# Value products of an attention in runs of two blocks

## The reference

```python
# attention a: one key and value head for all 16 query heads, D = 16
scores = jnp.einsum('bnhd,bmd->bhnm', q, k) / jnp.sqrt(jnp.float32(D))
attn = jax.nn.softmax(jnp.where(causal, -jnp.inf, scores), axis=-1)
out = jnp.einsum('bhnm,bmd->bnhd', attn, v).reshape(b, n, E) @ w_fc + b_fc
# attention b: own keys and values for each head, ALiBi
scores = jnp.einsum('bhqd,bhkd->bhqk', q, k) / scale + _alibi_bias(H, Tlen)[None]
out = jnp.einsum('bhqk,bhkd->bhqd', jax.nn.softmax(scores, axis=-1), v)
```

## Time and profile before

| | us |
|---|---|
| median of 3 runs | 1035.86 (1034.84 to 1036.69) |
| the profiled execution's own time | 1033.63 |
| its span | 1031.9 |
| busy in the span: TensorE, VectorE | 964.2 (93%), 760.6 (74%) |
| busy in the span: ScalarE, GpSimd | 570.4 (55%), 411.3 (40%) |

### The profile page before, as it was taken

How to read it: one execution, slowest core, us unless ns; L and a number is a source line. 1 busy time by engine, 2 the same in 40 slices (tenths; PEclk the granted TensorE clock), 3 DMA queues, 4 the chain that set the end, 5 groups by cost and what they waited for, 6 DMA issues and landing times.

```text
span 1031.9 us, 19370 instructions
## 1 busy us (share of the span) xinstructions
PE 964.2 (93%) x6370; PEld 613.2 (59%) x6370; DVE 760.6 (74%) x2132; ACT 570.4 (55%) x1078; POOL 411.3 (40%) x434
## 2 busy tenths in 40 slices
PE   4888999999889999999998989999999899999998
PEld 3433333333358889988886433333334588899887
DVE  6798999999256776447778979999992568764475
ACT  4525777777744335653354647777777533466332
POOL 3420634333435417625843102323225361374570
PEclk9879999999989999999999989999999999999999
DMA  4721212210105215733249523334401251266351
GB/s 142 193 46 30 47 44 44 44 44 9 49 26 203 80 47 173 181 122 120 67 116 218 118 36 69 61 70 77 76 13 44 84 173 53 82 190 160 117 183 48
DMA packets 66755, 95.40 MB, mean 92 GB/s; under 512 B 19669, under 2 KB 50821, under 8 KB 64599
## 3 DMA queue, kind: packets, MB, share of 16 engines
q1 hardware_dynamic: 46645, 52.74, 19.0%
q10 hardware_dynamic: 13100, 22.53, 8.6%
q0 software_dynamic: 6912, 18.88, 7.0%
HBM read 66.79 MB, written 26.67 MB: 91 GB/s over the span
## 4 chain that ended last, share of the span: by engine, by line
PE 71%; DVE 16%; issue 4%; DMA 3%; ACT 3%; POOL 2%; SPq 1%; ACTq 0%; DVEq 0%; POOLq 0%
PE o_ps L1101 13%; PE st_ps L1084 8%; PE su_ps L1043 7%; PE st_ps L293 7%; PE st_ps L294 7%; PE st_ps L295 7%; PE o_ps L1241 4%; PE st_ps L1043 4%; PE su_ps L1241 3%; DVE mab L1729 3%; PE su_ps L1147 3%; DVE unread L1725 3%; PE st_ps L1276 2%; DVE xn L1604 1%; PE su_ps L293 1%
## 5 line engine op out<-in xcount | busy, mean ns | idle before, releaser
L1446 ACT ACTIVATE pt<-st_ps 128x512 f32<-128x512 f32 (+1 forms) x584 | 312.0, 596 | 161.3 <-PE st_ps L1084 153.5
L1084 PE MATMUL st_ps<-qs,ks 99*128 99x512 bf16 (+9 forms) x768 | 211.8, 328 | 4.3 <-DMA qs<-nmx 2.4
L807 POOL TENSOR_SCALAR_AFFINE_SELECT pt<-pt 128x512 f32<-128x512 f32 x120 | 74.7, 641 | 311.7 <-ACT pt L1446 311.7
L1043 PE MATMUL su_ps<-ks,qs 102*128 102x512 bf16 (+7 forms) x538 | 155.2, 330 | 11.5 <-DVE mc L1725 4.5
L1101 PE MATMUL o_ps<-pt,vp 128*32 128x512 f32 (+3 forms) x1536 | 156.6, 505 | 0.0
L1725 DVE CUSTOM_DVE_ANT_0 unread<-su_ps,cst 128x384 f32<-128x384 f32 (+3 forms) x324 | 143.0, 479 | 16.2 <-PE su_ps L1043 15.5
L1729 DVE TENSOR_REDUCE mab<-su_ps 128x1 f32<-128x512 f32 (+2 forms) x181 | 118.6, 683 | 7.2 <-PE su_ps L1043 5.1
L1043 PEld LDWEIGHTS su_ps<-ks,qs 96*128 96x128 bf16 (+1 forms) x538 | 48.5, 98 | 122.4 <-DVE mab L1729 44.4
L888 POOL DMA_INDIRECT rows_in<-rows,source x80 | 79.1, 989 | 97.5 <-DVE source L1988 73.7
L1084 PEld LDWEIGHTS st_ps<-qs,ks 99*128 99x128 bf16 (+2 forms) x768 | 73.1, 98 | 63.5 <-ACT pt L1446 16.6
L1472 ACT CAST hh<-hf 128x512 fp32r<-128x512 f32 x64 | 39.7, 620 | 123.2 <-DVE hf L1943 123.2
(11 more groups left out here) (234 smaller groups left out, 1975.7 us busy)
## 6 DMA issues: line engine op xcount, KB each, us to landing
wu_raw<-w_units_dram SPq DMA_DIRECT2D x32, 384.0 KB, 3.2
outs<-rows_out ACTq DMA_DIRECT2D x40, 256.0 KB
q_parts<-hml SPq DMA_DIRECT2D x16, 384.0 KB, 3.1
wexp_raw<-w_units_dram SPq DMA_DIRECT2D x16, 384.0 KB, 6.5
inv<-inverses SPq DMA_DIRECT2D x128, 32.0 KB, 1.8
rows<-xn SPq DMA_DIRECT2D x8, 512.0 KB, 6.2
qs<-q_parts ACTq DMA_DIRECT2D x10, 384.0 KB
k_parts<-hml SPq DMA_DIRECT2D x8, 384.0 KB, 2.9
```

The lines of the kernel that those rows point to most:

```text
L807: pool.affine_select(block, block, [[0, 4], [1, P]], ALU.is_ge, 0.0, base=0, channel_multiplier=-1).then_inc(masked, 1)
L1043: last = pe.matmul(out_b[:, c0:c0 + width], query_columns(s, slice(0, rows), j0 + a, P * qt, P * qt + P), key_stack(l, s)(j0 + a)[0:rows, ...
L1084: last = pe.matmul(out_b[:, at:at + hi - lo], key_stack(l, s)(j)[0:rows, P * kt:P * kt + P], query_columns(s, slice(0, rows), j, lo, hi), ...
L1446: act.activation(exponentials(S, q)[:, j, 0:width_of(s, q)], bank[KM_BANKS[i % len(KM_BANKS)]][:, 0:width_of(s, q)], ACT.Exp, scale=1 / np ...
```

## The change

The value products are given in runs. Instead of one block at a time, two blocks behind the start of the piece, the order in each step is: block 0 alone behind block 2, blocks 1 and 2 behind block 4, 3 and 4 behind block 6, 5 and 6 behind block 8, and 7 and 8 behind block 1 of the next step, each time behind piece 1. In step 0, blocks 1 and 2 stay at the start of block 3, and 7, 8 and 9 come together at the start of block 10. The two copies of o_ps per step stand where the table of runs puts the last block of their half: the same places as before but in step 0, where both come one block earlier. Pieces, units and their plan stay as they are, and so does all of VectorE's and GpSimd's stream.

```diff
+def value_runs():
+    first = len(FIRST_BLOCKS)
+    runs = {2: (0,), 6: (3, 4), 8: (5, 6)}
+    early = {HALF_BLOCKS: (1, 2), first: (7, 8, 9)}
+    for s in range(1, STEPS):
+        for run in ((0,), (1, 2), (3, 4), (5, 6), (7, 8)):
+            runs[block_base(s) + run[-1] + PV_LAG] = tuple(block_base(s) + q for q in run)
+    return runs, early, runs.pop(block_base(STEPS) + PV_LAG - 1)
+
+RUNS, EARLY_RUNS, LAST_RUN = value_runs()
...
-                    if n in (HALF_PIECES, FIRST_PIECES):
-                        for early in range(i - PV_LAG, i):
-                            values(l, 0, early)
+                    if j == 0:
+                        for b in EARLY_RUNS.get(i, ()):
+                            values(l, *place_of_block(b))
                     key_major(l, s, q, j)
-                    if j == PV_BEHIND and i >= PV_LAG and i not in [*range(HALF_BLOCKS, HALF_BLOCKS + PV_LAG),
-                                                                    *range(len(FIRST_BLOCKS), len(FIRST_BLOCKS) + PV_LAG)]:
-                        values(l, *place_of_block(i - PV_LAG))
+                    if j == PV_BEHIND:
+                        for b in RUNS.get(i, ()):
+                            values(l, *place_of_block(b))
...
-                for q in range(len(LATER_BLOCKS) - PV_LAG, len(LATER_BLOCKS)):
-                    values(l, STEPS - 1, q)
+                for b in LAST_RUN:
+                    values(l, *place_of_block(b))
...
-                        if s and n == 4 * PV_LAG - 1:
+                        own = piece_base(s) + n
+                        if s and own == taking(block_base(s - 1) + last_of(s - 1, 1)[0]):
                             take_output(S - 1, 1)
-                        if n == 4 * (last_of(s, 0)[0] + PV_LAG + 1) - 1:
+                        if own == taking(block_base(s) + last_of(s, 0)[0]):
                             take_output(S, 0)
```

More of the change, by code:

```diff
@@ L161, in place_of_block, with run_behind, taking @@
     return next((s, i - block_base(s)) for s in reversed(range(STEPS)) if i >= block_base(s))
+def value_runs():
[6 more added lines that the diff above has]
+    return runs, early, runs.pop(block_base(STEPS) + PV_LAG - 1)
+PV_LAG = 2
+RUNS, EARLY_RUNS, LAST_RUN = value_runs()
+def run_behind(b):
+    return next((i for i, run in RUNS.items() if b in run), None)
+def taking(b):
+    i = run_behind(b)
+    if i is None:
+        i = next((i for i, run in EARLY_RUNS.items() if b in run), None)
+    return None if i is None else 4 * i + 3
 def unit_base(S):
@@ L224 @@
 FC_BEHIND = {10 + 3 * t: t for t in range(QT)}
-PV_LAG = 2
 PV_BEHIND = 1
```

## The result

The changed kernel takes 1058.02 us (median of 4 runs, 1054.0 to 1058.73) against 1035.35 us (4 runs, 1033.29 to 1036.69) for the kernel before on the same chip: ratio 1.0213, 95% interval 1.0182 to 1.0244. The forecast was 1062, between 1050 and 1072. It is slower, as forecast, by about 2%. The profiled execution took 1058.73 us, 25.1 more than that of before (1033.63); the sum had said 26.4.

A forecast was written before the change was run, and what follows sets the result against it. TensorE and VectorE in turns, with three banks between them, were taken to bound the kernel. Layer terms of +13.6 and +12.8 us on 1033.63 gave 1060.0; with the median 2.2 higher, 1062, range 1050 to 1072.

The forecast's parts named there:

- the sum: Both layers' terms together: +13.6 and +12.8 us, +26.4 on the profiled execution's 1033.63 us.
- The gap of a double run, 2.96 - D: VectorE's idle gap at two merged value-product blocks: 2.96 us less D, its work on three banked units.
- rival 2: In inner steps a double run leaves a gap of 0.8 us, not 1.2: some +10 us, 1046; chance 9%.
- +2.26 per step: Growth of VectorE's gaps in one inner step, in us: +0.36, +0.61, +0.43 and +0.86 for the four runs of two.
- block 1's, put at 0.10: VectorE's gap at single block 1 of an inner step before the change, too short for a bracket: 0.10 us assumed.
- TensorE's saved switches turn into waiting: In each inner step TensorE's 0.76 us saved by fewer switches into and out of value products becomes waiting.
- Step 0: Each layer's first step, runs 3, 4 and 5, 6: +0.8 us in layer 0, -0.2 in layer 1.
- The run of three: Blocks 7, 8, 9 of step 0 given together: +0.5 us in layer 0, +0.7 in layer 1, between -0.1 and +1.4.
- blocks 1 to 4 (+1.04): Runs 1, 2 and 3, 4 of step 1, in each layer's first interval between transposes of the maxima: +1.04 us.
- The last step: Each layer's last step, without score units: merges save 0.76 us, ScalarE's gaps grow; 0 taken, bounds -0.8 and +3.
- 1, TensorE keeps the saving: VectorE's waits overlap work it has anyway, so the time follows TensorE: 11 us less, 1025; chance 5%.
- 3, the clock falls behind the transpose: TensorE's clock halves behind each inner step's transpose of the maxima, slowing blocks 5, 6: +19 us, 1081; chance 6%.

The follow-up runs named there:

- pair56: Kernel before with only blocks 5 and 6 of each step made a run of two, all others single: 1040.14 us, ratio 1.0054.
- light_no56: Changed kernel with blocks 5 and 6 single again, VectorE's maxima reading a quarter of their columns and the exponent divided by 64: 995.63 us, ratio 0.9626.
- before_again: The kernel before, unchanged, run once more for its profile on the chip of the other kernels of that call: 1037.58 us (one run).
- light kernels: Kernel before and changed kernel, each with VectorE's maxima reading a quarter of their columns and the exponent divided by 64: ratios 0.9678 and 0.9699; light_no56 is the third.
- unit_first_runs: Changed kernel with TensorE's order from step 1 on turned to value products, unit, piece: 1058.27 us, ratio 1.021.
- both lag3: Kernel before with single blocks one block later: ratio 1.0229; the same with the maxima sent ahead of the sums on SyncE's queue: 0.9986.
- last_only: Kernel before with runs of two only in the last step of each layer: 1032.95 us, ratio 0.9974.
- last_sp: last_only with the maxima sent ahead of the sums on SyncE's queue: 1031.5 us, ratio 0.9963.
- both unit_first: Kernel before with the order value products, unit, piece from step 1 on: 1066.29 us, ratio 0.9979; the other is unit_first_runs.
- best: last_sp with the order value products, unit, piece from step 1 on: 1027.52 us, ratio 0.9929.

## Why the prediction was right, point by point

*The gap of a double run, 2.96 - D* (2.86 - D where the units on both sides have 384 columns; the prediction took that off without saying so for blocks 5 and 6): right. Predicted 1.16, 1.18, 1.13, 1.21 for blocks 7/8, 1/2, 3/4 and 5/6; measured, by starts, 1.16, 1.20 (0.17 of it a reciprocal), 1.14 and 1.21. Both changes made to its terms moved it as it says: pair56 alone +0.71 predicted and +0.70 measured, and a piece less on the path -0.22 at each gap. These are the test of the formula. Its agreement with the earlier trace rows tested nothing: there every term was the distance between two starts of the same rows, so that sum less D had to give the gap that the rows show, and rival 2 was weighed against an agreement that could not fail.

*+2.26 per step:* measured +2.06 (29.85 - 27.79). The gaps themselves changed by +2.27 (block 1's, put at 0.10, was 0.13). The missing 0.2 is VectorE's side: a wait of 0.15 right behind the chain at the transpose, which I had left out, went away, and the last few hundredths are VectorE's instructions, a little shorter than before. Over five steps and two layers that is 2 us of the sum.

*TensorE's saved switches turn into waiting:* right. Counted by starts, TensorE waits 4.9 us in the step of after and 1.97 in that of before, +2.9. The step's growth and the saving give 2.06 + 0.76 = 2.8. light_no56 shows the saving itself.

*Step 0:* mis-sized both ways. The run of three lies in a stretch at half clock (1.2 GHz, 99.3 to 106.1 and 621.6 to 628.4) in both layers. TensorE's timeline in layer 0, and VectorE's:

```profile
102.77 4.00 PE L1131 MATMUL o_ps<-pt,vp 128*32 128x384 f32 x32
```

```profile
107.35 0.69 DVE L1756 CUSTOM_DVE_ANT_0 unread<-su_ps,cst 128x512 f32<-128x512 f32 x1 [3.50 <-PE su_ps L1073]
```

The bracket of 1.94 became 3.50 and that of 2.71 became 3.96. The earlier trace rows showed the half clock there in layer 0, and by the prediction's own twice 0.9 at half clock, less 0.35, the term was 1.4; I took 0.5, the figure of the full clock. Net of blocks 1 to 4 (+1.04) the first interval grew by 1.5 in layer 0 and 1.3 in layer 1, predicted 0.5 and 0.7, above my bound of 1.4 in layer 0. Some of this is no part of the change: in before_again, the same kernel as before, that interval of layer 0 is 28.59 and not 28.00, with the half clock up to 107.0 in place of 103.2. The pairs before it cost +1.3 in layer 0 (predicted +0.8; some of it is a half-clock stretch from 72.0, longer by 3.4 us than before, and not of the change), and -1.0 in layer 1 (predicted -0.2).

*The last step:* the wait for the transfer (1.40 before) is gone in layer 0 and 0.20 in layer 1, which fits that it swallows what comes before it. From the last transpose to the end of the value products the time grew by 1.6 in layer 0 and 0.4 in layer 1, where I took 0 between -0.8 and +3. In layer 0 the clock fell there, after a run of its own:

```profile
280.20:283.60 3.40, 3.40 (x25) 0.98 (x18) 0.11 (x1) 0.90 (x2) 1.33 (x2) 0.50 0.39 115
```

```profile
280.00 3.48 PE L1131 MATMUL o_ps<-pt,vp 128*32 128x512 f32 x24
283.41 0.91 PE L1114 MATMUL st_ps<-qs,ks 99*128 99x512 bf16 x3
```

*The rivals.* 1, TensorE keeps the saving: it needs a VectorE with time to spare, which in the inner steps only the light kernels have, and block 5 behind the transpose beside (light_no56). 2, the gaps are 0.8: no. 3, the clock falls behind the transpose: in none of the ten inner steps of the change, but in three of unit_first_runs at 1.6 us each, so it was a real risk. The Trainium skill's "TensorE: Matmul & The Clock Gate", A second HAM failure mode, tells of a gate that goes back and forth when TensorE idles briefly and often between groups of matmuls. The traces agree in part at most: in unit_first_runs the clock fell once in each of three steps, and in the changed kernel, where TensorE waits for 4.9 us of each inner step in many short pieces, in none.

That the sum of 26.4 landed so near 25.1 is in part luck, since small misses lay on both sides: -2 in the inner steps, +1.6 in the first intervals, -0.3 before them, and +2 in the last steps; the other -2.7 lie between and behind the attentions, which the change does not touch. The bounds were added up wrong: with all of them one way (4, the last steps -1.6 to +6, 2) they reach from 1054 to 1074, and not to 1070.

## What to carry to other kernels

When two engines are both near full and meet in a few banks, as here, the length of each absence of the producer counts, and not only the sum of its work: price a merge as (issue of the last unit before it to start of the next one behind it) less the consumer's work in the banks, and compare it with the gaps that it replaces. Save switches where the consumer has time in hand, here in the last step. And before a block of filler work is moved, look at what chain it was lying over, and at which transfer stands in the queue behind what the move delays.

## What the runs showed of the hardware

- The same run of 24 value products took 1.93 us at the full clock and 3.33 to 3.48 us where the granted clock was 0.50.
- VectorE's CAST of 32x128 from fp32 to bf16 is as long as GpSimd's mask makes it. Twelve of the fourteen CASTs of each kernel start while a mask of 0.64 us runs. Where the mask ended 0.09 to 0.10 us after the CAST's start (the two main kernels, pair56, both lag3, last_only, last_sp), the CAST took 0.21; where it ended 0.46 to 0.50 after it (both unit_first, best, the three light ones), the CAST took 0.53 to 0.58 and ended 0.07 to 0.08 behind the mask, each time. The two without a mask beside them took 0.21 to 0.22 in every kernel. No run was made to move the mask alone.
- In unit_first_runs the granted clock fell from 1.00 to 0.50 in three of ten inner steps and held in the other seven, with the same order of instructions and with TensorE busy 2.5 of the 3.60 us in front in all ten.
